# A two-block image network on one Trainium2 core: the last image's row gathers use four buffers in turn in place of two

## The chip, the core and the metric

The program runs on one core of one Trainium2 chip. The core has a matrix engine (TensorE, PE in the profile), a vector engine (VectorE, DVE), an activation engine (ScalarE, ACT), GpSimd (POOL), which here issues the indirect DMAs, and SyncE (SP), which issues the plain DMAs. Sixteen DMA engines carry all transfers. The metric is the time of the whole program on the device in microseconds (us), lower is better.

## The reference, cut to what matters

Eight images of 56 x 56 tokens with 64 channels go through two blocks. The first block is a token mixer by squared similarities and a mixture of 16 experts. The second is a deformable 3 x 3 convolution, then a feed-forward layer that only the best half of an image's tokens get:

```
pos_y = base_y + inner_y + off_yx[..., 0]          # 9 taps a token, each at a learned place
v1..v4 = the four table cells around (pos_y, pos_x)
value = (hh*hw*v1 + hh*lw*v2 + lh*hw*v3 + lh*lw*v4) * mask
x = x + einsum('nhwc,cf->nhwf', value, w)          # the deformable convolution
...
weights = einsum('bsd,do->bso', ln(t), wr) + br
_, idx = top_k(weights, k)                         # the routed half
y = gelu(sel @ w1 + b1) @ w2 + b2, times weights   # for these tokens only
t = t + (ln(t) + y scattered)
```

The convolution's reads are the gathers: a token's tap needs four neighbouring cells, and the kernel keeps a table in DRAM whose row holds all four (4 x 64 floats).

## The kernel before, in words

An image's 3136 tokens are 25 tiles of up to 128 tokens (T = 25, the last tile has 64). `LAST` is image 7 and `PREV` image 6. For each image the program first writes the corner table (SP, `write_table`), then gathers tile by tile. A tile is nine indirect DMAs on GpSimd, one for each tap (L446 to L449), into one half of the buffer `G`; tiles take the halves in turn, by the parity of the running number n = 25 b + t. Before tile n GpSimd waits until tile n - 2 has left its half (`valued` at n - 1, L445).

VectorE's `weigh` (L477) waits for the nine gathers, then works in place: three multiplications by the corner weights (L486, pieces 0 to 2), one addition (L492) and one that writes `value` and counts up `valued` (L494). TensorE's `sample` transposes `value` and multiplies by the convolution's weights, with two copies by ScalarE (`sample_evac`) between, and VectorE adds the result to the image (`sample_add`, L499).

The images overlap. While image k is mixed and goes through its experts, the tiles of image k - 1 are gathered and sampled between its steps. Nothing comes after image 7, so its 25 tiles stand in a loop of their own at the end (VectorE L1185 to L1190, TensorE L1854 to L1874, ScalarE L1461 to L1480). Its order is written out by hand. In the loop, `beside(t)` puts other work behind tile t's `weigh`: for t = 0 to 2 the layer norm of image 6; for t = 4 to 7 the outputs of its feed-forward chunks (`tail_out`, L1133); from t = 7 to 19 the search for the threshold of the routed half of images 0 to 6 (`round_try`, `round_take`, `choose_end`); from t = 8 on the layer norm and feed-forward chunks of image 7 (`tail_norm`, `tail_out`); and for t = 20 to 24 the final sums of images 0 to 6 (`final_back(i)` at the tiles `LAST_FINAL`). After the loop come the last chunk, the threshold search for image 7 and its final sum.

For a final sum of image i, SP loads two arrays back from DRAM (`load_back`, L406 to L411), VectorE masks one and adds it to the other (L1096, L1098), and SP stores the result (L419). Two pairs of buffers are there (`fin_x`, `fin_y`), so `load_back(i + 2)` waits until image i is stored (L409).

The expert weights w1, w2 (each in two float16 parts) and w3 lie in five tensors of their own. Their last reader is the last chunk of image 7's experts, which counts up `ytm_done` to B x NCH = 56.

The gathers of a tile write 128 x 2304 floats, 9216 bytes in each partition.

## Time and profile before

| what | value |
|---|---|
| time, median of 3 runs | 4599.6 us (4589.3 to 4605.0) |
| the profiled execution's span | 4742.8 us |
| TensorE busy | 3689.9 us (78%) |
| VectorE busy | 3096.6 us (65%) |
| ScalarE busy | 2394.1 us (50%) |
| GpSimd busy | 1954.9 us (41%), 1800 gathers of 1086 ns |
| loop over image 7's tiles | from about 4268 to 4683 us |
| after it, to the end | 4683 to 4743 us |

The profile is one execution under the hardware profiler, and its span is 143 us longer than the median of the timed runs. Times inside it are microseconds from the first instruction. The row of an engine's instruction names its start, its length, the line, what it writes and reads, and in brackets how long the engine had been idle before and who ended that. For GpSimd a row is the issuing of one gather; the data comes later, on the DMA engines.

### The profile page before, as it was taken

To read this page: it belongs to the slowest core of one execution; us is meant where nothing else is said; L and a number is where in the kernel's file an instruction comes from. 1 tells how busy PE (TensorE), PEld (TensorE's weight loads), DVE (VectorE), ACT (ScalarE), POOL (GpSimd) and SP (SyncE) were. 2 spreads that over 40 slices of the span, in tenths; PEclk is the share of its full clock that TensorE was granted. 3 is DMA by queue.
4 is the path that set the end of the run, shared out by engine and by line. 5 is a ranking of instruction groups with operands and counts; after the bars stand their busy time and mean duration, and the time that the engine had idled before them with its cause. 6 is when DMAs were issued, how large, how long until landed. Compare 5 with 4: busy or idle time off the path is not lost.

```text
span 4742.8 us, 58643 instructions
## 1 busy us (share of the span) xinstructions
PE 3689.9 (78%) x21912; PEld 1953.7 (41%) x21912; DVE 3096.6 (65%) x4834; ACT 2394.1 (50%) x4144; POOL 1954.9 (41%) x1805
## 2 busy tenths in 40 slices
PE   6889868888788878889788888889788888864432
PEld 2334434444444444444444444444544444433421
DVE  5466457766677566766577567766577576664765
ACT  5656644466445654466445664456444664431210
POOL 0000344526255343535255353544345354446661
PEclk8999979999799978999799888989799988975555
DMA  3000222222122221222122221231222222233436
GB/s 99 8 1 1 73 59 60 65 66 79 51 65 68 70 72 57 67 73 71 51 65 66 70 77 55 64 86 51 55 71 72 71 71 57 60 89 89 111 97 125
DMA packets 374811, 314.93 MB, mean 66 GB/s; under 512 B 312672, under 2 KB 317024, under 8 KB 374528
## 3 DMA queue, kind: packets, MB, share of 16 engines
q0 software_dynamic: 85248, 231.33, 16.5%
q1 hardware_dynamic: 289280, 79.88, 7.9%
q8 instruction: 172, 2.82, 0.2%
q14 instruction: 111, 0.91, 0.1%
HBM read 279.30 MB, written 57.69 MB: 71 GB/s over the span
## 4 chain that ended last, share of the span: by engine, by line
PE 54%; DVE 14%; ACT 9%; another core or an unknown queue 9%; issue 7%; DVEq 3%; DMA 2%; POOL 2%; SPq 1%; ACTq 0%
PE PS L1487 49%; DVE work L866 3%; PE PS L1690 3%; DVEq L488 2%; ACT work L1379 2%; DVE G L492 2%; POOL G L448 2%; PE PS L1522 1%; ACT work L1308 1%; DVE G L486 1%; DVE st L454 1%; DVE small L862 1%; DVE work L777 1%; DMA out<-x 1%
## 5 line engine op out<-in xcount | busy, mean ns | idle before, releaser
L448 POOL DMA_INDIRECT G<-corner_table,index x1800 | 1954.3, 1086 | 2651.6 <-DVE value L494 1256.1
L1379 ACT ACTIVATE work<-PS,descale 128x512 f32<-128x512 f32 (+2 forms) x896 | 565.5, 633 | 638.0 <-PE PS L1487 510.6
L866 DVE SCALAR_TENSOR_TENSOR work<-PS,descale,work 128x512 f32<-128x512 f32 (+2 forms) x896 | 604.8, 681 | 385.0 <-ACT work L1379 276.1
L1308 ACT ACTIVATE work<-PS 128x768 f32<-128x768 f32 (+2 forms) x800 | 650.5, 823 | 374.3 <-PE PS L1487 251.0
L777 DVE TENSOR_TENSOR work<-work 128x768 f32<-128x768 f32 (+2 forms) x496 | 481.1, 973 | 440.2 <-PE PS L1487 280.3
L1487 PE MATMUL PS<-xn_hl,xn_hh 128*128 128x384 f16 (+2 forms) x1600 | 550.8, 345 | 121.8 <-ACT work L1308 76.3
L1487 PE MATMUL PS<-work,xm 128*64 128x400 f32 (+3 forms) x3200 | 642.1, 514 | 0.4 <-DVE work L777 0.4
L486 DVE TENSOR_TENSOR G<-G,corner_w 128x768 f32<-128x768 f32 x600 | 559.8, 951 | 55.9 <-DMA G<-corner_table,index 53.4
L1487 PE MATMUL PS<-xn_hl,xn_ll 128*128 128x384 f16 (+2 forms) x1600 | 546.7, 342 | 0.0
L1487 PE MATMUL PS<-work,w3s 128*64 128x384 f32 (+2 forms) x1792 | 466.8, 600 | 85.6 <-DVE small L862 80.8
L1487 PE MATMUL PS<-xn_hl,w1h 128*128 128x512 f16 (+2 forms) x896 | 331.1, 370 | 157.5 <-DVE work L866 131.3
L1385 ACT ACTIVATE small<-PS 128x512 f32<-128x512 f32 (+2 forms) x448 | 243.0, 542 | 253.1 <-PE PS L1487 195.8
L1487 PEld LDWEIGHTS PS<-xn_hl,xn_hh 128*128 128x128 f16 (+1 forms) x1600 | 160.7, 100 | 461.8 <-ACT work L1308 211.9
L1487 PE MATMUL PS<-xn_hl,w1l 128*128 128x512 f16 (+2 forms) x896 | 329.9, 368 | 0.0
L1487 PE MATMUL PS<-xn_hl,w2h 128*128 128x512 f16 (+2 forms) x896 | 328.3, 366 | 0.0
L1487 PE MATMUL PS<-xn_hl,w2l 128*128 128x512 f16 (+2 forms) x896 | 328.1, 366 | 0.0
L1487 PEld LDWEIGHTS PS<-work,xm 128*64 128x64 f32 (+1 forms) x3200 | 241.3, 139 | 200.8 <-issue 167.2
L862 DVE TENSOR_TENSOR small<-PS,small 128x512 f32<-128x512 f32 (+2 forms) x448 | 276.9, 618 | 55.0 <-PE PS L1487 34.6
L1232 ACT ACTIVATE val_cm<-PS 128x512 f32<-128x512 f32 x200 | 118.3, 592 | 329.0 <-PE PS L1522 241.5
L492 DVE TENSOR_TENSOR G<-G 128x1152 f32<-128x1152 f32 x200 | 271.8, 1359 | 18.1 <-issue 0.4
L1690 PE MATMUL PS<-ident,small 128*128 128x128 f32 x1600 | 262.3, 284 | 2.8 <-issue 1.8
L1337 ACT ACTIVATE work<-work 128x768 f32<-128x768 f32 (+3 forms) x304 | 259.7, 854 | 3.2 <-PE PS L1487 3.1
(258 smaller groups left out, 4959.1 us busy)
## 6 DMA issues: line engine op xcount, KB each, us to landing
G<-corner_table,index POOLq DMA_INDIRECT x1800
corner_table<-rows_scratch SPq DMA_DIRECT2D x32, 784.0 KB
corner_table<-G SPq DMA_DIRECT2D x8, 841.0 KB, 8.5
xin<-x SPq DMA_DIRECT2D x8, 768.0 KB, 5.3
rows_scratch<-xln SPq DMA_DIRECT2D x8, 768.0 KB
x_scratch<-xB SPq DMA_DIRECT2D x8, 768.0 KB
yw_scratch<-yw SPq DMA_DIRECT2D x7, 784.0 KB
x<-x_scratch SPq DMA_DIRECT2D x4, 784.0 KB
```

The costliest lines, as they stand in the source:

```text
L448: GP.indirect_dma_start(G[0:rows, n % 2, tap * 4 * C:(tap + 1) * 4 * C], None, tables[b % 2], bass.IndirectOffsetOnAxis(ap=index[0:rows, c ...
L486: V.tensor_tensor(g, g, bc(w, 2, C), ALU.mult)
L492: V.tensor_tensor(g[:, :, 0:2, :], g[:, :, 0:2, :], g[:, :, 2:4, :], ALU.add)
L777: V.tensor_tensor(sq[0:rows, u % 4, :, 0:n], relu[0:rows, u % 2, :, 0:n], relu[0:rows, u % 2, :, 0:n], ALU.mult).then_inc(s["sq_dve"], 1)
L862: V.tensor_tensor(scaled_y[:, p % 2, 0:w], Y0[:, 0:w], share[:, p % 2, 0:w], ALU.mult).then_inc(s["scaled_done"], 1)
L866: V.scalar_tensor_tensor(hid[:, e % 4, 0:w], S[2 + e % 2][:, 0:w], descale[:, MOE2:MOE2 + 1], silu[:, e % 2, 0:w], ALU.mult, ALU.mult).the ...
L1308: A.activation(relu[0:rows, u % 2, :, 0:n], PS[u % 2][0:rows, :, 0:n], ACT.Relu).then_inc(s["relu_done"], 1)
L1337: A.activation(sq[0:rows, u % 4, :, 0:n], relu[0:rows, u % 2, :, 0:n], ACT.Square).then_inc(s["sq_act"], 1)
L1379: A.activation(silu[:, e % 2, 0:w], S[e % 2][:, 0:w], ACT.Silu, scale=descale[:, MOE1:MOE1 + 1]).then_inc(s["silu_done"], 1)
L1385: A.activation(share[:, e // 2 % 2, 0:w], Y1[:, 0:w], ACT.Copy, scale=1.0 / XS).then_inc(s["share_ready"], 1)
L1487: return P.matmul(o, a, b, start=start, stop=stop, skip_group_check=True)
L1690: ins = P.matmul(D1[0:rows, n * 128:(n + 1) * 128], scaled_y[:, p % 2, n * TP:n * TP + rows], ident[:, :], start=p == 0 and n == 0, stop=p ...
```

## The change

The five expert tensors become slices of one tensor `experts_w` (the same 20480 bytes in each partition). `G_buffers` has four entries: the two halves of `G` and two stretches of 9216 bytes of `experts_w`. Images 0 to 6 gather as before. For image 7, tile t takes buffer (2, 3, 1, 0)[t % 4]: tiles 0 and 1 go to the expert weights, tiles 2 and 3 to the halves of `G`. GpSimd waits for the end of the last experts (`ytm_done`) before tiles 0 and 1, and before tile t >= 2 until tile t - 4 (for t = 2, 3 image 6's tiles 23 and 24) has left its buffer. Each buffer has a semaphore of its own, and `gathered` computes what to wait for.

```
@@
-        w1h = sb("w1h", [128, E * HID], f16)
...
-        w3s = sb("w3s", [HID, E, C])
+        WH = E * HID // 2
+        experts_w = sb("experts_w", [128, 4 * WH + E * C])
+        w1h, w1l, w2h, w2l = (experts_w[:, i * WH:(i + 1) * WH].bitcast(f16) for i in range(4))
+        w3s = experts_w[:, 4 * WH:4 * WH + E * C].rearrange("p (e c) -> p e c", c=C)
@@
         G = sb("G", [128, 2, 4 * TAPS * C])
+        GW = 4 * TAPS * C
+        G_buffers = (G[:, 0, :], G[:, 1, :], experts_w[:, 0:GW], experts_w[:, GW:2 * GW])
@@
-        gath = (s["gath0"], s["gath1"])
+        gath = (s["gath0"], s["gath1"], s["gath2"], s["gath3"])
@@
+        def gather_buffer(b, t):
+            return (b * T + t) % 2 if b < LAST else (2, 3, (PREV * T + T - 2) % 2, (PREV * T + T - 1) % 2)[t % 4]
+
+        def gathered(b, t):
+            n, q = b * T + t, gather_buffer(b, t)
+            before = 0 if b < LAST or q > 1 else (LAST * T + 1 - q) // 2
+            return (before + (n // 2 if b < LAST else t // 4) + 1) * (TAPS * 16)
@@ gpsimd
-                    n, rows = b * T + t, tile_rows(t)
-                    if n >= 2:
+                    n, rows, q = b * T + t, tile_rows(t), gather_buffer(b, t)
+                    if b == LAST and t < 2:
+                        pool.wait_ge(s["ytm_done"], B * NCH)
+                    elif b == LAST:
+                        pool.wait_ge(s["valued"], n - 3)
+                    elif n >= 2:
                         pool.wait_ge(s["valued"], n - 1)
...
-                        GP.indirect_dma_start(G[0:rows, n % 2, tap * 4 * C:(tap + 1) * 4 * C], None, tables[b % 2],
+                        GP.indirect_dma_start(G_buffers[q][0:rows, tap * 4 * C:(tap + 1) * 4 * C], None, tables[b % 2],
@@ weigh
-                q, u = (b * T + t) % 2, (b * T + t) // 2
-                g = G[0:TP, q, :].rearrange("p (n s c) -> p n s c", n=TAPS, s=4)
+                q = gather_buffer(b, t)
+                g = G_buffers[q].rearrange("p (n s c) -> p n s c", n=TAPS, s=4)
...
-                        dve.wait_ge(gath[q], (u + 1) * (TAPS * 16))
+                        dve.wait_ge(gath[q], gathered(b, t))
```

No engine instruction is added, removed or moved; where a gather writes and what is waited for change. On GpSimd the end of image 6's gathers (tile 24, 64 tokens) and the first two tiles of image 7's stand so before (each tile is one row that waits and one of eight more):

```order
L448 DMA G<-corner_table0,index 64x256 [waits valued]
L448 DMA G<-corner_table0,index 64x256 x8
L448 DMA G<-corner_table1,index 128x256 [waits valued,idx_ready,table_written]
L448 DMA G<-corner_table1,index 128x256 x8
L448 DMA G<-corner_table1,index 128x256 [waits valued]
```

and so in the changed kernel:

```order
L463 DMA G<-corner_table0,index 64x256 [waits valued]
L463 DMA G<-corner_table0,index 64x256 x8
L463 DMA experts_w<-corner_table1,index 128x256 [waits ytm_done,idx_ready,table_written]
L463 DMA experts_w<-corner_table1,index 128x256 x8
L463 DMA experts_w<-corner_table1,index 128x256 [waits ytm_done]
L463 DMA experts_w<-corner_table1,index 128x256 x8
L463 DMA G<-corner_table1,index 128x256 [waits valued]
```

The rows stand in the same order; the first two tiles wait for the experts in place of VectorE. On VectorE, tile 21 and the first final sum whose loads begin inside the loop stand so before:

```order
L486 TENSOR_TENSOR G<-G,corner_w 128x768 [waits gath0]
L486 TENSOR_TENSOR G<-G,corner_w 128x768 x2
L492 TENSOR_TENSOR G<-G 128x9x128
L494 TENSOR_TENSOR value<-G 128x576 [waits val_tr]
L499 TENSOR_TENSOR xB1<-xB1,PS3 128x64 [waits dcn_done]
L1096 TENSOR_TENSOR work<-work,sel 112x1792 [waits yw_back0,x3_back0]
```

and so in the changed kernel:

```order
L501 TENSOR_TENSOR experts_w<-experts_w,corner_w 128x768 [waits gath3]
L501 TENSOR_TENSOR experts_w<-experts_w,corner_w 128x768 x2
L507 TENSOR_TENSOR experts_w<-experts_w 128x9x128
L509 TENSOR_TENSOR value<-experts_w 128x576 [waits val_tr]
L514 TENSOR_TENSOR xB1<-xB1,PS3 128x64 [waits dcn_done]
L1111 TENSOR_TENSOR work<-work,sel 112x1792 [waits yw_back0,x3_back0]
```

Only the buffer and its semaphore differ. `yw_back0` and `x3_back0` are the landings of the two arrays that SP loads for a final sum.

## Rows read from the trace of the kernel before

**Rows 1.** The page: the profiled execution's span.

```profile
span 4742.8 us, 58643 instructions
```

**Rows 2.** Waits from 4268 to 4743: us in total, times, longest.

```profile
POOL G L448 <- DVE value L494: 63.5, 14, 15.6
...
DVE G L486 <- DMA G<-corner_table,index: 23.0, 4, 6.8
```

**Rows 3.** Timeline of DVE: tiles 4, 5 (with its end), 17 and 18 of image 7.

```profile
4333.14 2.70 DVE L486 TENSOR_TENSOR G<-G,corner_w 128x768 f32<-128x768 f32 x3 [6.62 <-DMA G<-corner_table,index]
...
4359.76 2.69 DVE L486 TENSOR_TENSOR G<-G,corner_w 128x768 f32<-128x768 f32 x3
...
4363.96 0.76 DVE L494 TENSOR_TENSOR value<-G 128x576 f32<-128x576 f32 x1
...
4541.18 2.69 DVE L486 TENSOR_TENSOR G<-G,corner_w 128x768 f32<-128x768 f32 x3
...
4552.32 2.69 DVE L486 TENSOR_TENSOR G<-G,corner_w 128x768 f32<-128x768 f32 x3
```

**Rows 4.** Timeline of POOL, image 7: first or last gathers of tiles.

```profile
4268.38 1.06 POOL L448 DMA_INDIRECT G<-corner_table,index  x1 [20.49 <-issue]
...
4330.43 0.95 POOL L448 DMA_INDIRECT G<-corner_table,index  x1 [0.30 <-issue]
...
4354.62 0.94 POOL L448 DMA_INDIRECT G<-corner_table,index  x1 [0.30 <-issue]
4364.98 0.94 POOL L448 DMA_INDIRECT G<-corner_table,index  x1 [9.42 <-DVE value L494]
...
4374.96 0.94 POOL L448 DMA_INDIRECT G<-corner_table,index  x1 [0.30 <-issue]
...
4546.42 0.96 POOL L448 DMA_INDIRECT G<-corner_table,index  x1 [0.30 <-issue]
...
4573.82 0.94 POOL L448 DMA_INDIRECT G<-corner_table,index  x1 [1.72 <-issue]
...
4600.32 2.62 POOL L448 DMA_INDIRECT G<-corner_table,index  x1 [15.55 <-DVE value L494]
...
4618.41 0.95 POOL L448 DMA_INDIRECT G<-corner_table,index  x1 [0.30 <-issue]
...
4636.46 0.90 POOL L448 DMA_INDIRECT G<-corner_table,index  x1 [5.18 <-DVE value L494]
...
4648.54 0.90 POOL L448 DMA_INDIRECT G<-corner_table,index  x1 [0.30 <-issue]
```

**Rows 5.** The chain that ended last, 4604 to 4680: start, us, what.

```profile
4613.61 13.66 DMA out<-xin
...
4630.57 11.96 DMA out<-x
...
4645.59 10.69 DMA out<-xin
...
4659.42 9.36 DMA out<-x
```

**Rows 6.** DMA queues in the four stretches of rows 5, in order.

```profile
q0 software_dynamic: 528, 1.44, 37.9%
...
q0 software_dynamic: 240, 0.59, 18.5%
...
q0 software_dynamic: 160, 0.33, 15.1%
...
q1 hardware_dynamic: 7544, 1.92, 116.3%
```

**Rows 7.** Timelines of PE, DVE and ACT around 4350: image 7's tile 4.

```profile
4346.92 1.06 PE L1522 MATMUL PS<-ident,value 128*128 128x128 f32 x4
...
4358.71 0.28 DVE L1139 TENSOR_SCALAR w_all<-PS,descale,brc 112x4 f32<-112x4 f32 x1 [15.93 <-remote]
...
4358.77 0.60 ACT L1232 ACTIVATE val_cm<-PS 128x512 f32<-128x512 f32 x1 [14.94 <-remote]
```

More of the change, by code:

```diff
@@ L94, in metaformer_kernel @@
         w_mix = sb("w_mix", [C, C])
-        w1h = sb("w1h", [128, E * HID], f16)
-        w1l = sb("w1l", [128, E * HID], f16)
-        w2h = sb("w2h", [128, E * HID], f16)
-        w2l = sb("w2l", [128, E * HID], f16)
-        w3s = sb("w3s", [HID, E, C])
+        WH = E * HID // 2
+        experts_w = sb("experts_w", [128, 4 * WH + E * C])
+        w1h, w1l, w2h, w2l = (experts_w[:, i * WH:(i + 1) * WH].bitcast(f16) for i in range(4))
+        w3s = experts_w[:, 4 * WH:4 * WH + E * C].rearrange("p (e c) -> p e c", c=C)
         gateh = sb("gateh", [128, E], f16)
@@ L201, in metaformer_kernel @@
             fup_done gelu_done fdown_done fout_read tdown_done tout_read yw_done skip_added x3_stored yw_stored
-            count_in count_done tie_in tie_done x3_back0 x3_back1 yw_back0 yw_back1 bias_zero ident_loaded fin_ready out_stored0
+            count_in count_done tie_in tie_done gath2 gath3 x3_back0 x3_back1 yw_back0 yw_back1 bias_zero ident_loaded fin_ready out_stored0
             out_stored1""".split()}
-        gath = (s["gath0"], s["gath1"])
+        gath = (s["gath0"], s["gath1"], s["gath2"], s["gath3"])
         BODIES, GROUP = 2 * BPH, 14
@@ L447, in _ @@
                         col = t * TAPS + tap
-                        GP.indirect_dma_start(G[0:rows, n % 2, tap * 4 * C:(tap + 1) * 4 * C], None, tables[b % 2],
-                                              bass.IndirectOffsetOnAxis(ap=index[0:rows, col:col + 1], axis=0)).then_inc(gath[n % 2], 16)
+                        GP.indirect_dma_start(G_buffers[q][0:rows, tap * 4 * C:(tap + 1) * 4 * C], None, tables[b % 2],
+                                              bass.IndirectOffsetOnAxis(ap=index[0:rows, col:col + 1], axis=0)).then_inc(gath[q], 16)
         @block.vector
@@ L477, in weigh @@
             def weigh(b, t, piece):
-                q, u = (b * T + t) % 2, (b * T + t) // 2
-                g = G[0:TP, q, :].rearrange("p (n s c) -> p n s c", n=TAPS, s=4)
+                q = gather_buffer(b, t)
+                g = G_buffers[q].rearrange("p (n s c) -> p n s c", n=TAPS, s=4)
                 if piece < 3:
                     if piece == 0:
-                        dve.wait_ge(gath[q], (u + 1) * (TAPS * 16))
+                        dve.wait_ge(gath[q], gathered(b, t))
                     n = 4 * TAPS // 3
-                    g = G[0:TP, q, :].rearrange("p (n c) -> p n c", c=C)[:, piece * n:(piece + 1) * n, :]
+                    g = G_buffers[q].rearrange("p (n c) -> p n c", c=C)[:, piece * n:(piece + 1) * n, :]
                     w = corner_w[:, :, :].rearrange("p n s -> p (n s)")[:, t * (4 * TAPS) + piece * n:t * (4 * TAPS) + (piece + 1) * n]
```

## The prediction, made before the changed kernel ran

> **What bounds the kernel now.** The change touches only the last loop, image 7's 25 tiles, so I read the waits from its first gather (4268) to the end, then the timelines of VectorE and GpSimd beside each other, then the chain that ended last. The waits say two things that seem to disagree [rows 2]. GpSimd stood idle 63.5 us in 14 places because a buffer was not yet free: that is the wait the change takes away. VectorE, for whom the gathers are made, waited for gathered data only 23.0 us in 4 places. An engine that is early everywhere gives nothing when it gets earlier, so the question is where these four places lie, and whether a free buffer would have ended them.
>
> They all lie before tile 5: the fourth and last is tile 4 at 4333.14, 6.62 us [rows 3]. In that stretch GpSimd never waited for a buffer. It issued from 4268.38 to 4355.56 (the row at 4354.62 and its 0.94) without a pause, seven tiles of nine gathers, 12.5 us a tile, and its first wait for `value` stands ahead of 4364.98, at tile 7 [rows 4]. The four waits are for GpSimd's rate, and the start at 4268.38 is set by the indices, not by a buffer (the releaser there is not `value`). From tile 5 on (4359.76, no wait) VectorE finds its data there each time. The place where two buffers are nearest to binding is tiles 17 and 18, 11.14 us apart, the closest in the loop [rows 3]; tile 18's last gather was issued by 4547.38 [rows 4], 4.9 us before VectorE took it at 4552.32, of which the landing takes a part.
>
> The loop's end is different. From 4604 to 4680 the chain goes through DMA: store an image, load two arrays for the next but one, add, store. Four of its pieces are stores of one size, and they shrink: 13.66, 11.96, 10.69 and 9.36 us [rows 5].
>
> **The change part by part.** *Joined expert tensors.* The same bytes, the same instructions, the same operands' shapes: nothing, 0 us.
>
> *The wait for `ytm_done` before tiles 0 and 1.* The experts end before image 7's own layer norm and offsets, whose indices set 4268.38 [rows 4]. GpSimd waits for the indices anyway and nothing else is queued behind it: 0 us. If that cover were gone, each microsecond would show at tile 0, which VectorE waits for.
>
> *The waits for `valued`, two tiles looser.* I laid the gathers out again with the old times of VectorE. Tiles 0 to 6 stay, since GpSimd is busy all along. Tile 7 starts at about 4355.9 in place of 4364.98, and 8, 9 and 10 follow without a pause, up to some 4401. From there GpSimd has caught up and starts when VectorE frees a buffer, at the same moments as before, but for the tile two further on. So the slots of the issue times stay and the tiles shift: 4573.82 holds tile 23 in place of 21, 4600.32 holds tile 24 in place of 22, and the slots at 4618.41 (tile 23) and 4636.46 to 4649.44 (tile 24) [rows 4] are empty. VectorE gains nothing by the earlier tiles themselves, since none was late after tile 4.
>
> *What the two empty slots free.* Here the gathers share the 16 DMA engines with the chain. Their packets took 37.9% of the engines' time in the first of the four stretches, 18.5% and 15.1% in the next two, and none in the fourth, where only the plain queue has a row [rows 6]. In time of all engines that is 5.2, 2.2 and 1.6 us, and the stretches are 4.3, 2.6 and 1.3 us longer than the fourth [rows 5]: 0.8 to 1.2 us of path for each microsecond of gather. So I take the excess over 9.36 as the gathers' price. In the second and third stretch all gathers go: 2.6 + 1.3 = 3.9 us. In the first, the packets are those of 11 gathers (528 packets, 48 each). Five belong to the slot that began at 4600.32 and remain, but that slot now holds tile 24, which has 64 tokens in place of 128 and so half the bytes. What remains is then 2.5 of 11, and 8.5/11 x 4.3 = 3.3 us goes. The sum is 3.3 + 3.9 = **7.2 us**, on the path, since the rest of the loop and the end hang on the last load. Its bounds: nothing, if the stores shrink for a reason of their own; and 8.2 us x 1.2, some 10 us, if all gather time in these stretches goes at the dearer rate. I take 7.2, as three stretches agree in one rate.
>
> What the Trainium skill says on this, in DMA: Bandwidth & Descriptors, section Issuing engines are not separate DMA queues, is that transfers started by GpSimd and by SP run on the same 16 engines and interleave. The shares and lengths above agree with that.
>
> *What is late next.* The final sums of images 2 to 6 still wait for their loads, and their work on VectorE is the same; tile 24's data is there before tile 22 is worked on. Nothing else comes near the chain before the last load has landed.
>
> The sum against the profiled execution: 4742.8 [rows 1] - 7.2 = 4735.6 us. The timed median is 143 us below that span; the stores and gathers are not instructions of the engines that the profiler slows visibly, so I carry the 7.2 us over: 4599.6 - 7.2 = **4592.4 us**.
>
> **The rivals.** *Nothing moves.* The stores get shorter because later ones overlap less with each other, not because gathers go. For it: the plain queue alone has 116.3% of the engines in the last stretch [rows 6], so packets overlap, and a share is no exact measure. Against it: each stretch holds the same three transfers. It gives 4599.6 us.
>
> *Slower: TensorE is held while gathers run.* At tile 4 the transposes of `value` were issued by 4348 (4346.92 + 1.06), but ScalarE and VectorE, which both waited for TensorE, were released together at 4358.7, by nothing that the profile shows, after 14.9 and 15.9 us [rows 7]. The gathers' long row had ended at 4355.56, 3.1 us before [rows 4]. If TensorE's results are held back until a run of gathers ends, then a longer run costs. With the change, tiles 7 and 8 follow without a pause: two more tiles of 11.2 us (4364.98 to 4375.90, and a gap), 22.4 us, after which GpSimd must wait for tile 5's `value`. That makes 22.4 - 7.2 = +15.2 us, 4614.8 us. It decides only if the hold lasts to the end of the run. Against it: the run had then gone on for 80 us while TensorE's earlier tiles came through without such a delay, and the timed runs are 143 us shorter than the profile, so part of such holds may belong to the profiler. I give it one in ten.
>
> The Trainium skill, SBUF — State Buffer, section Who interferes with whom, says that DMA never contends with a compute engine and that TensorE waits on nobody. By it this rival is void. The coincidence of the two ends above speaks against that, and no row here settles it.
>
> *Faster by more than the sum.* The timed runs lack the holds, so VectorE would reach its tiles sooner, find gathers late, and four buffers would then save a wait. The price: two buffers bind if VectorE comes back sooner than a gather takes. A tile's nine gathers take 10.9 us to issue [rows 4] and about 2 to land (tile 4's last gather was issued by 4331.38 and VectorE took it at 4333.14) [rows 3, 4], 13 us from the freeing of the buffer. At the closest spacing, 11.14 us, the second tile after begins 2 x 11.14 - 4.96 = 17.3 us after the freeing, where 4.96 is one tile's work on VectorE (4359.76 to 4364.72) [rows 3]. There are 4 us to spare, so it would need ten tiles closer than that by 1 us each to reach 10 us more, 4582 us. Unlikely.
>
> **How the numbers follow.** A measurement of this kernel can tell about 0.3% from no change, which is 13.8 us: 4585.8 to 4613.4. Forecast (gathers out of the stores' way, 4592.4): 0.60. Nothing moves (4599.6): 0.20. Held TensorE (4614.8): 0.10. Faster by more (4582): 0.10. The first two are within the bound but for scatter; the three runs before span 15.7 us, and a median of the forecast can fall below 4585.8, for which I move 0.04 over. So faster 0.14, same 0.76, slower 0.10. The range takes in the forecast and no change with the scatter of runs, 8 us below the first and 10 above the second, and leaves out most of the two outer rivals: 4584 to 4610.
>
> **What the profile of the changed kernel would show.** GpSimd's issues run on from 4268 to about 4400 with no wait for `value` before tile 10 or so, then wait as before. The last gather is issued near 4618 in place of 4649. The first three stores on the chain take 10.3, 9.4 and 9.4 us in place of 13.66, 11.96 and 10.69. VectorE's waits for gathers stay four, all before tile 5, and stay near 23 us. If the stores keep their lengths, the rate was wrong. If the releases at 4358.7 and after move back by 10 us or more while GpSimd runs on, the held TensorE is real, and if VectorE waits for gathers after tile 4, the layout of slots was.

## The result: slower by a third of a percent, and where the time went

The changed kernel takes 4603.6 us in the median of 20 runs (4565.4 to 4625.8), the kernel before 4587.4 us (4571.1 to 4605.0). The ratio is **1.0034, with a 95% interval from 1.0017 to 1.005**: 16 us slower, where 7 us faster had been forecast. In some groups of runs below the kernel before takes 4587 to 4594 us, in others 4706 to 4718, so each ratio compares runs of one group only. The first profile of before [rows 1] was of the longer kind; the one of after has a span like its timed runs:

```profile
span 4600.7 us, 58643 instructions
```

Image 7's first gather starts 148.2 us earlier in it than in [rows 4], so its times are compared as distances from there. The waits from that gather to the end (us in total, times, longest), beside [rows 2]:

```profile
ACT val_cm L1247 <- remote: 55.0, 4, 31.6
...
DVE w_all L1154 <- remote: 49.5, 4, 32.5
...
POOL G L463 <- DVE value L509: 26.8, 7, 9.9
...
POOL experts_w L463 <- DVE value L509: 19.9, 6, 9.7
...
DVE experts_w L501 <- DMA experts_w<-corner_table,index: 17.7, 3, 6.8
...
DVE G L501 <- DMA G<-corner_table,index: 5.6, 1, 5.6
```

GpSimd waits less for buffers (46.7 us in place of 63.5), and VectorE waits for gathers as before (23.3 us, 4 times, all before tile 5). What has grown are the waits called "remote", in which VectorE and ScalarE wait for a semaphore that the profile can put down to nobody. From 4268 to 4743 in the trace of before they were:

```profile
ACT val_cm L1232 <- remote: 40.3, 4, 14.9
DVE w_all L1139 <- remote: 35.0, 4, 15.9
```

The longest of each has about doubled, and both end at one place. First GpSimd's timeline (start, length, line, operation, idle time before and its releaser):

```profile
4120.14 1.06 POOL L463 DMA_INDIRECT experts_w<-corner_table,index  x1 [20.47 <-issue]
...
4242.54 0.95 POOL L463 DMA_INDIRECT experts_w<-corner_table,index  x1 [0.30 <-issue]
4253.37 0.95 POOL L463 DMA_INDIRECT G<-corner_table,index  x1 [9.88 <-DVE value L509]
```

Ten tiles (90 gathers) go in one run of 123.4 us, where before it were seven (63) in 87.2 us. Now the same stretch on TensorE, VectorE and ScalarE:

```profile
4216.99 3.25 PE L1502 MATMUL PS<-f2s,work 128*112 128x64 f32 x16 [1.45 <-ACT work L1466]
4220.03 1.06 PE L1537 MATMUL PS<-ident,value 128*128 128x128 f32 x4
4249.19 0.48 PE L1541 MATMUL PS<-ident,value 128*128 128x128 f32 x1 [28.10 <-ACT val_cm L1247]
...
4247.10 0.28 DVE L1154 TENSOR_SCALAR w_all<-PS,descale,brc 112x4 f32<-112x4 f32 x1 [32.55 <-remote]
...
4248.54 0.60 ACT L1247 ACTIVATE val_cm<-PS 128x512 f32<-128x512 f32 x1 [31.61 <-remote]
```

TensorE's rows say that a block of 16 float32 instructions (a feed-forward chunk's second layer, called the f2s block below) and the four transposes behind it were over by 4221.1. The engines that wait for the two are released at 4247.1 and 4248.5, 3.6 and 5.1 us after GpSimd's run ended. The ends of matmuls are modelled in such a page; the releases are not. In slices of 10 us (busy us and instructions of PE, weight loads, DVE, ACT and POOL, then the granted clock, the DMA share and GB/s):

```profile
4220.00:4230.00 10.00, 1.09 (x6) 0.69 (x5) 0.00 (x0) 0.00 (x0) 7.57 (x8) 0.50 0.36 105
4230.00:4240.00 10.00, 0.00 (x0) 0.00 (x0) 0.00 (x0) 0.00 (x0) 7.57 (x8) 0.50 0.36 105
```

Three engines do nothing while GpSimd issues gathers that nobody needs yet. I call this a hold. It is not all that this run did: of the f2s blocks that met it earlier, the one at 4192.74 had ScalarE released 11.3 us after its start, where 4.1 us is usual with no gather about (e6), while GpSimd ran on for 39 us more. The chain of work that ended last shows it too, and then the stores that answer to [rows 5]:

```profile
4216.93 31.58 another core or an unknown queue
...
4477.52 11.41 DMA out<-xin
...
4491.99 10.35 DMA out<-x
...
4505.36 9.21 DMA out<-xin
...
4517.51 9.26 DMA out<-x
```

The table puts the pieces together. An interval is the time from the end of one tile's `value` to the next one's on VectorE; the last column goes from tile 0's to the end of the program. It holds one profiled execution of each kernel, the experiments below among them.

| kernel | 4 | 5 | 6 | 7 | 8 | 9 | 10 | 20 | 22 | 23 | tile 0 to end |
|---|---|---|---|---|---|---|---|---|---|---|---|
| before | 11.7 | 26.6 | 18.4 | 19.1 | 14.0 | 16.2 | 13.8 | 26.5 | 23.1 | 27.1 | 456.4 |
| before, second profile (e0) | 12.0 | 30.1 | 19.1 | 16.9 | 18.9 | 16.2 | 13.8 | 26.6 | 22.8 | 27.5 | 464.1 |
| after | 11.8 | 17.4 | 45.5 | 19.1 | 14.0 | 16.2 | 13.8 | 20.6 | 21.9 | 22.7 | 462.4 |
| after, second (e4) | 13.9 | 46.7 | 19.0 | 14.8 | 15.3 | 16.2 | 13.8 | 20.9 | 21.4 | 22.2 | 464.6 |
| e1 all waits tight | 11.7 | 26.6 | 17.6 | 19.1 | 14.0 | 16.2 | 13.8 | 26.5 | 23.2 | 27.0 | 455.7 |
| e2 loose from 12 | 12.1 | 30.6 | 19.2 | 16.9 | 17.1 | 16.3 | 13.8 | 26.5 | 22.6 | 22.3 | 477.2 |
| e3 loose up to 11 | 11.7 | 43.8 | 25.7 | 19.2 | 14.0 | 16.0 | 13.8 | 26.5 | 22.5 | 27.9 | 480.3 |
| e5 loose from 19 | 12.0 | 27.8 | 18.3 | 18.3 | 14.6 | 16.3 | 13.8 | 53.3 | 22.9 | 22.1 | 478.8 |
| e6 no gathers 4 to 10 | 5.3 | 17.4 | 15.8 | 15.8 | 14.7 | 16.3 | 13.8 | 20.9 | 21.4 | 23.2 | 424.5 |
| e7 memsets 4 to 10 | 5.2 | 15.9 | 10.3 | 10.3 | 9.6 | 16.3 | 13.7 | 19.6 | 21.2 | 22.7 | 405.6 |
| e16 long memsets | 24.9 | 19.4 | 19.4 | 19.4 | 19.3 | 19.4 | 19.4 | 46.0 | 22.2 | 22.6 | 499.5 |
| e9 half the rows | 11.3 | 52.7 | 19.1 | 19.1 | 14.1 | 16.2 | 13.8 | 26.6 | 21.5 | 22.5 | 476.5 |
| e10 a quarter of the bytes | 11.4 | 52.2 | 18.3 | 18.4 | 14.6 | 16.3 | 13.8 | 29.4 | 21.8 | 22.1 | 477.7 |
| e11 plain DMAs | 7.3 | 13.9 | 10.3 | 10.3 | 9.6 | 16.3 | 20.9 | 26.6 | 22.3 | 22.1 | 419.8 |
| e12 gaps | 21.2 | 15.6 | 15.6 | 15.6 | 20.4 | 18.5 | 14.7 | 45.5 | 21.1 | 22.9 | 476.8 |
| e13 few one-column matmuls | 11.8 | 13.3 | 27.0 | 41.5 | 14.7 | 16.2 | 13.8 | 20.9 | 22.0 | 21.7 | 462.9 |
| e14 short f2s blocks | 11.7 | 13.0 | 13.1 | 13.0 | 16.0 | 16.3 | 49.3 | 20.9 | 22.4 | 22.3 | 457.6 |
| e8 pauses | 11.9 | 13.8 | 16.3 | 14.9 | 15.7 | 17.5 | 25.3 | 19.2 | 19.6 | 28.2 | 444.7 |
| e15 pauses, one more | 12.6 | 17.9 | 16.3 | 15.3 | 17.3 | 16.3 | 16.3 | 18.9 | 20.4 | 27.7 | 439.6 |
| e17 the pauses on two buffers | 11.8 | 13.9 | 16.3 | 15.0 | 17.3 | 17.5 | 16.0 | 18.8 | 19.8 | 28.6 | 437.4 |

After against before: tiles 5 to 7 took 82.0 us in place of 64.1 (+17.9), tile 20 20.6 in place of 26.5 (-5.9), tiles 22 and 23 44.6 in place of 50.2 (-5.6). That is +6.4 of the +6.0 us that the last column shows.

One profile is one draw, so each term has to be seen in the others too. The first stands: intervals 5 to 8 add up to 77 to 85 us in the five profiles whose waits are tight there (before, e0, e1, e2, e5), and to 96 to 103 in the three with loose ones and all work done (after, e4, e3). So does the last: interval 23 is 27.0 to 27.9 where the end is tight (before, e0, e1, e3) and 22.1 to 22.7 where it is loose (after, e4, e2, e5). Tile 20's term isn't the change's. Where GpSimd neither paused for tile 20 nor was in a long run at its block, the interval is 26.5 to 29.4 us in the eight profiles with spans above 4660 us (before is one of them) and 19.6 to 20.9 in the six with spans below 4610 us (after is one). Without it the profiles give +17.9 - 5.6, some 12 us as an estimate; the timed runs say +16, with an interval from 8 to 23. The last column alone would not show it: e0 has 464.1 us, more than the kernel after.

### The profile page after: what moved, and what is told of

Its sections match the earlier page's. It is cut to its first block, busy times and chain, and to the rows that moved or that the text cites. A ratio compares the mean times of both kernels' runs of the same rounds, so it can differ in the third digit from the quotient of the medians.

```text
span 4600.7 us, 58643 instructions
## 1 busy us (share of the span) xinstructions
PE 3659.8 (80%) x21912; PEld 1953.1 (42%) x21912; DVE 3094.1 (67%) x4834; ACT 2397.7 (52%) x4144; POOL 1975.0 (43%) x1805
## 3 DMA queue, kind: packets, MB, share of 16 engines
q0 software_dynamic: 85248, 231.33, 17.3%
## 4 chain that ended last, share of the span: by engine, by line
PE 59%; DVE 14%; ACT 9%; issue 7%; another core or an unknown queue 5%; DVEq 3%; DMA 2%; SPq 1%; POOL 1%; ACTq 0%
PE PS L1502 54%; DVE work L881 3%; PE PS L1705 3%; DVEq L503 2%; ACT work L1394 2%; DVE G L507 2%; PE PS L1537 2%; DVE small L877 1%; DVE G L501 1%; ACT work L1323 1%; DVE st L469 1%; DMA out<-x 1%; ACT small L1367 1%; ACT xn_hh L1441 1%
## 5 line engine op out<-in xcount | busy, mean ns | idle before, releaser
L463 POOL DMA_INDIRECT G<-corner_table,index x1683 | 1842.7, 1095 | 2390.5 <-DVE value L509 1057.5
L1502 PE MATMUL PS<-xn_hl,experts_w 128*128 128x512 f16 (+2 forms) x3584 | 846.2, 364 | 137.2 <-DVE work L881 110.6
L501 DVE TENSOR_TENSOR G<-G,corner_w 128x768 f32<-128x768 f32 x561 | 524.9, 951 | 36.9 <-DMA G<-corner_table,index 31.5
L1502 PE MATMUL PS<-work,experts_w 128*64 128x384 f32 (+2 forms) x1792 | 454.8, 586 | 81.5 <-DVE small L877 74.7
L1502 PEld LDWEIGHTS PS<-xn_hl,experts_w 128*128 128x128 f16 x3584 | 345.9, 103 | 405.0 <-DVE work L881 159.8
L507 DVE TENSOR_TENSOR G<-G 128x1152 f32<-128x1152 f32 x187 | 254.1, 1359 | 17.1 <-issue 0.4
L1537 PE MATMUL PS<-ident,value 128*128 128x128 f32 x800 | 139.1, 302 | 136.2 <-DVE xB L514 107.5
L1502 PE MATMUL PS<-ident,split 128*128 128x128 f16 (+1 forms) x1224 | 145.1, 255 | 114.1 <-DVE split L1145 35.8
```

The source lines that it names most:

```text
L463: GP.indirect_dma_start(G_buffers[q][0:rows, tap * 4 * C:(tap + 1) * 4 * C], None, tables[b % 2], bass.IndirectOffsetOnAxis(ap=index[0:row ...
L501: V.tensor_tensor(g, g, bc(w, 2, C), ALU.mult)
L507: V.tensor_tensor(g[:, :, 0:2, :], g[:, :, 0:2, :], g[:, :, 2:4, :], ALU.add)
L1502: return P.matmul(o, a, b, start=start, stop=stop, skip_group_check=True)
```

## The experiments

Each ratio is to the kernel before in the same group of runs, with its 95% interval. "Tight" is the old wait (`valued` at n - 1), "loose" the new one (n - 3).

**Splitting the change.** e1 keeps the four buffers and the joined tensor and only goes back to the tight wait; e2 is tight up to tile 11, e3 loose up to tile 11; e0 is the kernel before.

```
 e1  pool.wait_ge(s["valued"], n - 1)
 e2  pool.wait_ge(s["valued"], n - 1 if t < 12 else n - 3)
 e3  pool.wait_ge(s["valued"], n - 3 if t < 12 else n - 1)
```

> The changed kernel with its four buffers, but from tile 2 of image 7 on GpSimd waits as before for tile t-2 (valued at n-1), so that only tiles 0 and 1 may go early. If the buffers and the joined expert tensor cost nothing and the long unbroken run of gathers (4120.1 to 4243.5 in the profile after) is what costs, this takes the time of the kernel before: ratio 1.000, between 0.998 and 1.0015, and TensorE's semaphores in tile 5 come within about 12 us as before, not 28 to 32. If something else costs (the buffers' place in the expert tensor, other semaphores, the wait for ytm_done), it stays near 1.0034.

> The changed kernel with the old wait (valued at n-1) for tiles 2 to 11 of image 7 and the new one (n-3) from tile 12 on. If the early, long run costs and the empty slots at the end give, as the traces say (stores on the last chain 13.66, 11.96, 10.69 us before, 11.41, 10.35, 9.21 after, 5.4 us together), only the gain is left: ratio 0.9988, between 0.997 and 1.000. If the end gives nothing, 1.000.

> The other half: the new wait (n-3) for tiles 2 to 11, the old one (n-1) from tile 12 on. The theory that TensorE is held by the long run expects the cost alone without the gain of the end: the change's +16 us and the 5 us that it no longer gives back, +21 us, ratio 1.0045, between 1.003 and 1.006. If the early run costs nothing, 1.000. e2 and e3 together should add up to the change's 1.0034.

> The kernel before, once more, for a second profile: its first profiled execution had a span of 4742.8 us, 142 us above the one of the kernel after, while the timed runs differ by 16 us the other way. If that execution was out of the ordinary, this one has a span near 4590 us, and its waits of VectorE and ScalarE on TensorE at tile 4 to 7 of image 7 can be compared with those after. If the profiler lengthens this kernel each time, it is near 4740 again.

Measured: e1 1.0013 (0.9991 to 1.0034), e2 1.0024 (1.0004 to 1.0044), e3 1.0066 (1.0038 to 1.0095). e0's span was 4742.4 us, again longer than the median of its group, 4706.0. So the joined tensor and the four buffers cost nothing that shows: e1 has the intervals of before, though its timed interval alone reaches up to 1.0034. The early half does cost, a little more than its range said, and e2 and e3 together (0.90%) don't add up to the change's 0.34%. **e2 missed**: the late half was to be a gain and is a loss. Its end is as cheap as hoped (interval 23: 22.3 in place of 27.0), but tiles 11 to 18 were gathered in one run of 102 us, and tile 14 took 30.8 us in place of 13.7. A hold isn't a matter of the first tiles.

**The same, once more and later.** e4 is the changed kernel; e5 is loose only from tile 19 on.

```
 e5  pool.wait_ge(s["valued"], n - 1 if t < 19 else n - 3)
```

> The changed kernel once more, timed beside the kernel before on the chip of this group: the yardstick for the three others. Between 1.0017 and 1.006, as the first comparison gave 1.0034 and its early half alone 1.0066 on a chip on which TensorE was held longer.

> The changed kernel, but GpSimd waits as before (valued at n-1) up to tile 18 and by the new rule (n-3) from tile 19 on. With the new rule from tile 12 on, a run of gathers from tile 13 to 18 went on without a pause and TensorE's semaphores came late through it, some 30 us in tile 13. From tile 19 on TensorE has little to do, so the theory of the hold expects no new hold and the end's gain kept: 4.5 to 5 us, ratio 0.999, between 0.997 and 1.0005. If what costs is the earlier issue as such, whatever TensorE does, it is slower than 1.001.

Measured: e4 1.0067 (1.0039 to 1.0095), just above its range, e5 1.0067 (1.0041 to 1.0092). **e5 missed badly**, and shows why. TensorE and GpSimd around tile 20 of e5:

```profile
4405.95 3.25 PE L1502 MATMUL PS<-f2s,work 128*112 128x64 f32 x16 [0.32 <-issue]
4408.99 1.06 PE L1537 MATMUL PS<-ident,value 128*128 128x128 f32 x4
4445.19 0.47 PE L1541 MATMUL PS<-ident,value 128*128 128x128 f32 x1 [35.14 <-ACT val_cm L1247]
...
4438.71 0.95 POOL L463 DMA_INDIRECT G<-corner_table,index  x1 [0.30 <-issue]
4460.74 2.57 POOL L463 DMA_INDIRECT experts_w<-corner_table,index  x1 [21.09 <-DVE value L509]
```

An f2s block starts at 4405.95 in a run of gathers that ends at 4439.7, and nothing that waits for TensorE goes on before that. In the profile after, the same block (4442.34) started when a run had just ended (4442.14, followed by a pause of 1.72 us): interval 20.6 against 53.3. In the trace of before it stood in just the same place, 0.20 us behind a run's end at 4572.11 and with the same pause. The blocks and ScalarE's next work, before and after:

```profile
4572.31 3.25 PE L1487 MATMUL PS<-f2s,work 128*112 128x64 f32 x16 [0.32 <-issue]
4583.32 0.60 ACT L1232 ACTIVATE val_cm<-PS 128x512 f32<-128x512 f32 x1 [11.06 <-remote]
...
4442.34 3.25 PE L1502 MATMUL PS<-f2s,work 128*112 128x64 f32 x16 [0.32 <-issue]
4448.21 0.60 ACT L1247 ACTIVATE val_cm<-PS 128x512 f32<-128x512 f32 x1 [5.91 <-remote]
```

ScalarE was released 11.0 and 5.9 us after the block's start, where 4.1 is usual. So to start behind a run avoids the long hold, but what the nine gathers after it cost differs, and the position doesn't say why.

In e5 and in the profile after, the long hold lasts for what is left of the run when the block meets it: 33.7 us in e5, 26.5 in the profile after (from 4216.99). That is no rule: e2, e9, e10 and e12 have others.

**Without gathers, and without DMA.** e6 leaves out the gathers of tiles 4 to 10; e7 has GpSimd write zeros instead; e16 writes them five times.

```
e6, for tiles 4 to 10 in place of the gathers:
    GP.memset(G_buffers[q][0:1, 0:1], 0.0).then_inc(s["gsub"], 1)
e7:
    for tap in range(TAPS):
        ins = GP.memset(G_buffers[q][0:rows, tap * 4 * C:(tap + 1) * 4 * C], 0.0)
    ins.then_inc(s["gsub"], 1)
e16:
    for tap in range(TAPS):
        for _ in range(5):
            ins = GP.memset(G_buffers[q][0:rows, tap * 4 * C:(tap + 1) * 4 * C], 0.0)
            pool.drain()
    ins.then_inc(s["gsub"], 1)
```

> The changed kernel without the gathers of tiles 4 to 10 of image 7 (work left out; one element is set instead, and VectorE weighs what the buffers hold). If TensorE is held by gathers in flight, the holds of tiles 4 to 7 vanish: the 28 us before TensorE's semaphore in tile 5 and the smaller ones beside it, so it is faster than the kernel before by its own holds there (about 15 to 25 us) and than the changed one by 35 to 50: ratio 0.995, between 0.992 and 0.998. If the holds belong to TensorE's own work (its dense bursts, its instruction loading), they stay and the ratio is 1.003.

> The same, but for each left-out gather GpSimd writes zeros into the same 128 x 256 floats itself (nine such instructions a tile), so that GpSimd is busy, and writes the same bytes, but no DMA is started. If it is the descriptors and the data of the DMAs that hold TensorE, there is no hold and the time is that without gathers, within 5 us. If a busy GpSimd alone holds TensorE, the holds come back: near 1.003.

> The kernel of e7 (the gathers of tiles 4 to 10 left out, GpSimd writes zeros instead), but each of the nine writes of a tile is done five times, one after the other. In e7 a tile's writes took 2.34 us in all, so GpSimd was mostly idle; now they take at least 11.7 us, as long as nine gathers. If a GpSimd that is busy without a pause holds TensorE, an interval of 30 us or more comes back between tiles 4 and 10 and the ratio is 1.000 or more. If only DMAs that GpSimd describes do it, no TensorE semaphore is more than 2 us late there: ratio 0.992 to 0.998.

Measured: e6 0.9918 (0.9886 to 0.9951), just beyond its range, e7 0.9953 (0.9929 to 0.9977), 16 us slower than e6 where 5 had been allowed, e16 1.0113 (1.0082 to 1.0144). With no gather about, tiles 5 to 8 take 15 to 17 us each and TensorE works almost without a break:

```profile
4170.00:4180.00 10.00, 9.69 (x52) 7.93 (x50) 2.46 (x6) 2.89 (x4) 0.09 (x1) 0.50 0.00 1
4180.00:4190.00 10.00, 8.79 (x43) 7.29 (x43) 5.89 (x9) 2.32 (x4) 0.09 (x1) 0.50 0.01 2
```

So the holds come from the gathers, and the kernel **before** had them too: 26.6 + 18.4 + 19.1 us in tiles 5 to 7 against 17.4 + 15.8 + 15.8. e7 left GpSimd idle most of the time (2.34 us of writes a tile) and decided little; its 10.3 us a tile can't be compared with e6's 15.8, since its granted clock was 1.00 from 4180 to 4210. e16 decides it. Its ratio missed the expectation for two reasons. Each tile's writes took 19.4 us, so VectorE waited for them (intervals 4 to 10: 21 us more than before). And the gathers that came behind went without a pause from 4424.2 to 4588.5 and held tile 20's block (4562.17; interval 46.0, 20 us more). But GpSimd wrote without a pause from 4289 to 4423 us, and five f2s blocks (4294.89, 4300.45, 4319.41, 4324.97, 4338.85) passed in the part up to 4345 with no semaphore more than 2 us late:

```profile
4336.05 27.37 POOL L465 MEMSET G<- 128x256 f32 x64 [0.23 <-issue]
...
4330.00:4340.00 10.00, 7.16 (x33) 5.69 (x34) 3.31 (x9) 2.32 (x4) 7.20 (x24) 0.50 0.01 3
```

A GpSimd that is busy for 134 us doesn't hold TensorE here; the gathers do.

**Which part of a gather.** In tiles 4 to 10 of the changed kernel e9 gathers 64 rows in place of 128, e10 rows of 64 floats in place of 256, and e11 has GpSimd issue plain DMAs of the same size.

```
 e9   GP.indirect_dma_start(G_buffers[q][0:64, tap * 4 * C:(tap + 1) * 4 * C], None, tables[b % 2],
                            bass.IndirectOffsetOnAxis(ap=index[0:64, col:col + 1], axis=0)).then_inc(gath[q], 16)
 e10  GP.indirect_dma_start(G_buffers[q][0:rows, tap * 4 * C:tap * 4 * C + C], None,
                            tables[b % 2].rearrange("e (s c) -> (e s) c", c=C),
                            bass.IndirectOffsetOnAxis(ap=index[0:rows, col:col + 1], axis=0)).then_inc(gath[q], 16)
 e11  GP.dma_start(G_buffers[q][0:rows, tap * 4 * C:(tap + 1) * 4 * C],
                   tables[b % 2][tap * 128:tap * 128 + rows, :]).then_inc(gath[q], 16)
```

> The changed kernel, but the gathers of tiles 4 to 10 of image 7 bring 64 rows in place of 128 (part of the work left out): as many gathers, half the descriptors and bytes. If the data or descriptors of the DMAs hold TensorE in proportion, the hold at tile 5 or 6 is half as long, 15 us, and the ratio near 0.999. If what counts is that gathers follow each other without a pause, the hold still ends with the run: as long as before (about 30 us), ratio 1.003 to 1.006.

> The changed kernel, but each row that the gathers of tiles 4 to 10 bring has 64 floats in place of 256 (part of the work left out): the same gathers and descriptors, a quarter of the bytes. If the data written to SBUF holds TensorE, the hold shrinks to under 10 us and the ratio to 0.997. If it is the descriptors or their issue, it stays about 30 us, 1.003 to 1.006.

> The changed kernel, but GpSimd issues for tiles 4 to 10 plain DMAs of the same 128 x 256 floats from consecutive table rows, without a list of indices (part of the work left out). If any DMA that GpSimd starts and describes itself holds TensorE, the hold stays; if only the indirect ones do, it is gone, and the ratio is near the one without gathers, 0.992 to 0.997.

Measured: e9 1.0045 (1.0017 to 1.0073), e10 1.0036 (1.0006 to 1.0067), e11 0.9964 (0.9942 to 0.9986). Half the rows or a quarter of the bytes shorten no hold: interval 5 is 52.7 and 52.2 us, where the longest interval with all rows and bytes was 43.8 to 46.7 (e3, after, e4). In e10's hold the DMA engines were 12% busy, a third of the share in the kernel after, and everybody waits all the same:

```profile
4340.00:4350.00 10.00, 0.00 (x0) 0.00 (x0) 0.00 (x0) 0.00 (x0) 7.56 (x9) 0.50 0.12 26
```

With plain DMAs the holds are gone from these tiles, though the engines carry three times the traffic while they run (the DMA share is 1.02):

```profile
4293.63 9.64 POOL L463 DMA_DIRECT2D G<-corner_table  x18
...
4290.00:4300.00 10.00, 7.48 (x37) 5.58 (x35) 6.47 (x9) 4.64 (x7) 10.00 (x20) 0.50 1.02 325
```

They are also issued in half the time (0.53 us each, not 1.25), so e11's runs are short, and it doesn't show that a long run of plain DMAs is harmless. When the gathers came back behind tile 10, a block in their first run was late again (4357.94, ScalarE released 8.1 us after its start in place of 4.1; interval 10: 20.9 in place of 13.8). What e9 to e11 exclude is the traffic as the cause.

Nor was TensorE waiting for instructions to be loaded, a rival that e6's expectation names: the two queues that load them moved no packet in the holds of before at tile 4 (4344 to 4370), of after (4217 to 4250), of e5 (4400 to 4446) and of e14 (4240 to 4290), the releases included.

**Which of TensorE's instructions.** In image 6's chunks e13 does 2 of 8 one-column matmuls, e14 2 of 8 of the f2s matmuls.

```
 e13  for t in range(1 if f == PREV else CT):
          for w in (wrh, wrl):
 e14  for t in range(1 if f == PREV else CT):
          for m in range(2):
```

> The changed kernel, but each feed-forward chunk of image 6 does 2 of its 8 one-column matmuls that weigh the tokens (work left out). If a burst of these tiny instructions is what meets the gathers and starts the hold, the long hold at tile 5 or 6 goes: ratio 0.998 or less. If it starts in the block behind them, it stays: 1.003 to 1.007.

> The changed kernel, but each feed-forward chunk of image 6 does 2 of its 8 float32 matmuls by f2s (4 of 16 instructions; work left out). In each long hold the first late semaphore is that of this block. If the block of 16 starts the hold, it goes or shrinks to under 10 us, ratio 0.995 to 0.998 (TensorE also saves 2.4 us in each of seven chunks). If not, the ratio stays at 1.001 or more.

Measured: e13 1.0005 (0.9979 to 1.0031), e14 1.0006 (0.9980 to 1.0031). The ratios tell little, and e13's is under its expectation although its hold stayed (41.5 us in interval 7). e14's trace tells more: its run of gathers went on without a pause from 4104.4 to 4278.3, seven chunks with short blocks passed through it with no semaphore more than 2.3 us late, and behind the first full block, that of image 7's first chunk, TensorE stood still for 36 us:

```profile
4170.62 1.01 PE L1502 MATMUL PS<-f2s,work 128*112 128x64 f32 x4 [0.16 <-issue]
...
4244.70 3.25 PE L1502 MATMUL PS<-f2s,work 128*112 128x64 f32 x16 [0.86 <-issue]
4247.73 1.06 PE L1537 MATMUL PS<-ident,value 128*128 128x128 f32 x4
4284.54 0.48 PE L1541 MATMUL PS<-ident,value 128*128 128x128 f32 x1 [35.74 <-ACT val_cm L1247]
...
4277.34 0.95 POOL L463 DMA_INDIRECT experts_w<-corner_table,index  x1 [0.30 <-issue]
4295.46 2.17 POOL L463 DMA_INDIRECT G<-corner_table,index  x1 [17.17 <-DVE value L509]
```

It is one profile, so this points to the block of 16 and doesn't prove it, the less so as full blocks can pass too (below). And a short delay needs no f2s block: in e1, among image 6's tiles, ScalarE was released at 4173.08, 5.9 us after four transposes had started (4167.15) beside float16 matmuls of 128x448, where 1.1 us is usual; GpSimd's run had ended at 4170.51.

**Does a pause help?** e12 puts some 3.5 us without a gather ahead of each of the tiles 4 to 10 and keeps the loose waits.

```
+ if b == LAST and 4 <= t <= 10:
+     GP.memset(G_buffers[q], 0.0)
+     pool.drain()
```

> The changed kernel with its loose waits, but ahead of each of the tiles 4 to 10 of image 7 GpSimd sets the free buffer to zero and waits for that to be done, some 2.5 to 3 us in which it issues no gather (the gathers then overwrite it, so nothing else changes). If a hold of TensorE lasts until the gathers first pause, it now ends with the tile that it meets: at most some 13 us in place of 27 to 34 in one piece, the interval that is 46 us in the changed kernel falls to 30 or less, and the ratio to 0.999 to 1.001. If only the end of the whole run frees TensorE, or the bytes of these tiles, the interval stays over 40 us and the ratio at 1.004 or more.

Measured: 1.0052 (1.0022 to 1.0082). The ratio missed, the intervals did not: tiles 5 to 7 take 15.6 us each, the pace of the gathers with their gap, and none is held. But a gap ahead of tile 4, whose data VectorE was waiting for, costs 9 us at once, and past tile 10, where no gap was, a run from 4280.8 to 4458.7 met tile 20's block (interval 45.5 in place of 20.6 to 26.5). Rows of e12, VectorE waiting for tile 4's data and then for TensorE, and in between one of the full blocks in that run which nothing held:

```profile
4195.29 2.70 DVE L504 TENSOR_TENSOR experts_w<-experts_w,corner_w 128x768 f32<-128x768 f32 x3 [16.12 <-DMA experts_w<-corner_table,index]
...
4380.06 3.25 PE L1505 MATMUL PS<-f2s,work 128*112 128x64 f32 x16 [0.32 <-issue]
4384.20 0.60 ACT L1250 ACTIVATE val_cm<-PS 128x512 f32<-128x512 f32 x1 [4.19 <-PE PS L1540]
...
4467.04 0.17 DVE L1087 TENSOR_SCALAR kf<-PS 112x7 f32<-112x7 f32 x1 [31.74 <-PE PS L1505]
```

Five full blocks met this run. Three passed (ScalarE released 4.1 us after their start), one was 4 us late (4345.10), and only the last (4432.35) was held to the run's end. So a full block in a long run may be held and need not be.

**Pauses where TensorE's blocks are.** e8 and e15 use four buffers, tight up to tile 21, and let GpSimd also wait for TensorE; e17 has the same waits on the kernel before, with two buffers.

```
+ if 6 <= t <= 9:  pool.wait_ge(s["tdown_done"], min(2 * (t - 5), NCH))
+ if t == 11:      pool.wait_ge(s["tdown_done"], NCH + 1)      # e15, e17, not e8
+ if t == 21:      pool.wait_ge(s["tie_done"], 1)
  e8, e15:  pool.wait_ge(s["valued"], n - 3 if t >= 22 else n - 1)
  e17:      pool.wait_ge(s["valued"], n - 1)
```

> Four buffers, but GpSimd pauses where TensorE's feed-forward chunks run: image 7's tiles 2 to 21 wait for valued at n-1 as before, tiles 6 to 9 also until 2, 4, 6 and 7 chunks of image 6 are done (tdown_done), tile 21 until the ties are counted (tie_done), and tiles 22 to 24 go by the new rule (n-3). If TensorE's feed-forward block stays held until the run of gathers that it meets has ended, the intervals of tiles 5, 6 and 7 fall from 26.6, 18 and 18 us to about 17 each, that of tile 20 from 26.5 to 20.6 (as in the profile after), and the end gives 5: some 20 us together, ratio 0.9955, between 0.993 and 0.998. If the holds are no matter of where a run ends, pausing only makes tiles late: 1.002 or more.

> The kernel with pauses once more, and one pause added: tile 11's gathers also wait until the first chunk of image 7 is done. Without it, tiles 8 to 11 were gathered in one run of 51 us, and TensorE's chunk in it was held 13.6 us (the interval of tile 10 was 25.3 us in place of 13.8). The theory expects 13.8 there again and 11.5 us less in all: ratio 0.9952, between 0.9925 and 0.9975. If the hold only moves to another tile, it stays at 0.9976.

> The kernel before, with its two buffers and its tensors as they were, and only the pauses of e15 added: GpSimd waits for chunks ahead of tiles 6 to 9 and 11, for the ties ahead of tile 21. If e15's gain (0.996) is that of the pauses, this has it all but the two empty slots at the end (3 to 5 us): ratio 0.997, between 0.995 and 0.999. If the four buffers are needed for it, 1.000 or more.

Measured: e8 0.9976 (0.9952 to 1.0), e15 0.9960 (0.9933 to 0.9988), **e17 0.9944 (0.9919 to 0.9969)**, a little better than its range. e15 and e17 beat the kernel before with all of its work done. In e8 one hold was left, in a catch-up run of tiles 8 to 11 (interval 10: 25.3); e15's added wait took it away (16.3). GpSimd in e17, released by TensorE:

```profile
4359.05 0.94 POOL L454 DMA_INDIRECT G<-corner_table,index  x1 [2.28 <-PE PS L1493]
4374.04 0.94 POOL L454 DMA_INDIRECT G<-corner_table,index  x1 [2.18 <-PE PS L1493]
```

The waits ahead of tiles 6 to 9 and 11 save 12.1 us in e17's profile against before (intervals 5 to 10: 96.0 in place of 108.1), the one ahead of tile 21 another 6.9 (intervals 20 to 24). e17 needs none of the change: the pauses give the gain, not the buffers. Not every block is kept out of a run: in e17 the one at 4444.74 met a run with 28.1 us left and passed with the usual 4.1 us. The end's gain isn't in e8 and e15 either (interval 23: 28.2 and 27.7); with tile 21 paused the last gathers come later again, up to 4598.9 in e8, beside the stores.

## The prediction, step by step

*Joined tensors, the wait for `ytm_done`: 0.* Right (e1).

*The layout of gathers.* Right but for one tile. Tiles 0 to 9 went in one run, 123 us long; I had 0 to 10 in some 133 (4401 less 4268.4). Tile 10 had to wait for VectorE, which was itself held. GpSimd's last gather was issued 361 us after the first where I had 350. VectorE's waits for gathers are four, 23.3 us, all before tile 5.

*The two empty slots, -7.2 us.* The mechanism is right, the size a little large. The three stores went from 13.66, 11.96 and 10.69 us [rows 5] to 11.41, 10.35 and 9.21, together -5.3 us; I had written 10.3, 9.4 and 9.4. The rate was too high for the second: no gather's packet moved beside it any more, and it still took 1.1 us more than the fourth (9.26). One bound was also mislabelled: the 8.2 us there are the stores' excess, while the gathers' time in the three stretches adds up to 9.0.

*What is late next: nothing.* **This is the step that failed.** I asked which data or buffer would be late and found none, so the longer run itself stood in the sum at 0. But a longer run of gathers is a thing that TensorE's block can meet, and it met it: the run was 36 us longer (ten tiles for seven), the longest wait of VectorE for TensorE went from 15.9 to 32.6 us, and tiles 5 to 7 took 17.9 us more. The sign that I had set for it came: the hold that ended 90 us behind the first gather (4358.7) now ends 127 us behind it (4247.1). This is the rival *TensorE is held while gathers run*. It was priced at +22.4 for two more tiles, less the end's 7.2, and given 0.10. Measured were 17.9 for three more tiles, less 5.6 at the end.

That 4603.6 us lies inside the range of 4584 to 4610 is luck: the range was drawn around a small gain and no change, and a loss of 16 us fitted in.

*Why it got so little.* I had two arguments against it. "The run had then gone on for 80 us while TensorE's earlier tiles came through": true, but the tiles before have no f2s block; the first come at 4335.19 and 4343.88 in the trace of before, and the second is the one whose semaphore came at 4358.7 [rows 7]. That a long hold needs such a block is what e14 points to. "The timed runs are 143 us shorter than the profile, so part of such holds may belong to the profiler": the profile after is as long as its timed runs and has the longest hold of the two. The coincidence of the ends in [rows 4] and [rows 7] was the evidence, and it should have had about half the chance.

*Not foreseen at all:* that a run of gathers can meet a block late in the loop as well. In e5 it costs tile 20 some 33 us over the 20.6 of the profile after.

*The Trainium skill*, SBUF — State Buffer, section Who interferes with whom, says that DMA doesn't contend with a compute engine and that TensorE waits on nobody; by it the rival was void. For these indirect DMAs the runs say otherwise: with them interval 5 or 6 is 44 to 53 us in e3, e4, e9, e10 and the kernel after, without them (e6) 17.4 and 15.8. The page speaks of ports of the on-chip memory, and that fewer rows or bytes shorten no hold (e9, e10) doesn't speak against it there; which path it is stays open. The other page of the Trainium skill that I used, DMA: Bandwidth & Descriptors, section Issuing engines are not separate DMA queues, agrees with the stores, which got shorter when the gathers left.

**What stays open.** The runs tell that indirect DMAs issued without a pause and a block of TensorE together can make a hold, not by which path, and not which of the blocks is held: full blocks passed unheld in long runs of gathers in e2 (4416.65), e8 (4345.21), e12 and e17. Nor do all holds last to the run's end: in e2 ScalarE's two waits of tile 13 ended some 6 us late each (4457.03, 4465.52), and the run went on for 19 us behind VectorE's late one (4471.82); in e9 VectorE was released 7 us before the run's end; in e10 a first hold ended in the middle of a run and a second followed. That a long run of plain DMAs would do the same wasn't tried, nor gathers issued by fewer, larger instructions. Nor is it known why tile 20's interval differs by 6 us between profiles with long and with short spans, or why the loss is 0.67% in e4's group (about 31 us) and 0.34% in the first.

## What to carry to other kernels

When a wait is loosened, ask what the engine that is set free will run beside, and for how long without a break; "it is never waited for" says only that its own results aren't late. When two engines are released at one moment by nobody, and a third one's long burst ended just before, treat that as a cause and test it (leave the burst out) before trading on it. And a producer that is far ahead can be worth slowing: waits ahead of six tiles that keep GpSimd off most of TensorE's blocks gained 0.56% (0.31 to 0.81), where two more buffers lost 0.34%. Last, before a difference between two profiles is put down to the change, look whether it follows the change through all profiles: tile 20's 5.9 us did not.

## What the hardware showed that I had not expected

- TensorE's semaphores came up to 35 us late while GpSimd issued gathers back to back (e14: a block over by 4247.9 in the trace, TensorE's next work at 4284.54), with the DMA engines 35% busy, and also with 12% (e10).
- Full f2s blocks beside 134 us of GpSimd's memsets (e16), or beside plain DMAs at 102 and 76% of the DMA engines (e11, at 4299.31 and 4304.86), were not held.
- Full f2s blocks in a long run of gathers were held for 27 us (e12, 4432.35) or not at all (e12, 4380.06, in the same run).
- TensorE's granted clock is 0.50, its lower level of 1.2 GHz, from tile 1 to tile 10 in the profiles of before, after and e6. In e11 it was 0.50 from 4290 to 4300 (TensorE 75% busy), 0.80 in the next 10 us (85%) and 1.00 (2.4 GHz) from 4310 on, and a tile with two chunks then took 10.3 us in place of 15.8 in e6. In e6 there was no hold either, TensorE was busy 88 to 97% of each 10 us from 4150 to 4200, and the clock stayed at 0.50. What makes the difference isn't shown. A slice of e11:

```profile
4320.00:4330.00 10.00, 7.57 (x71) 6.38 (x68) 6.64 (x12) 3.56 (x6) 4.77 (x9) 1.00 0.39 118
```
